# Attention products taken key tile by key tile, with the four engines' call sequences written anew, in a decoder layer on one Trainium2 core

## What is computed

```python
q, k = _l2norm(q * SCALE) * sqrt(SCALE), _l2norm(k) * sqrt(SCALE)
sim  = jnp.einsum('bhid,bjd->bhij', q, k)
attn = jax.nn.softmax(sim, axis=-1)
out  = jnp.einsum('bhij,bjd->bhid', attn, v)       # 16 heads, one k and one v
out  = out.transpose(0, 2, 1, 3).reshape(B, N, HEADS * DIM_HEAD) @ Wout
```

## Time and profile before

| | us |
|---|---|
| median of 3 timed runs | 1501.87 |
| lowest, highest of them | 1498.53, 1508.65 |
| the profiled execution's own time | 1485.55 |
| its span, first to last instruction | 1483.7 |

### The profile page before, as it was taken

One profiled execution on the slowest core, in us unless ns is written; L12 is line 12 of the kernel. 1 busy time (PEld: TensorE's weight loads), 2 busy tenths in 40 slices (PEclk: granted clock), 3 DMA queues, 4 the chain that ended last, 5 costly groups with the idle time before them and its releaser, 6 DMA issues.

```text
span 1483.7 us, 26467 instructions
## 1 busy us (share of the span) xinstructions
PE 1326.2 (89%) x6890; PEld 1021.6 (69%) x6891; DVE 1117.6 (75%) x1545; ACT 936.8 (63%) x2450; POOL 466.5 (31%) x367
## 2 busy tenths in 40 slices
PE   4699999999999999999999899998931689999996
PEld 4378885548898554889855488985421578888885
DVE  4488599959888994988899498887775347776763
ACT  4668885368878546887853688784230347666663
POOL 0001001000044211134421103461404675666664
PEclk9889999999999999999999999999965789999998
DMA  7449988632687953268796326868721369999983
GB/s 276 194 129 276 270 207 235 159 108 65 167 239 175 241 148 108 63 167 244 169 241 155 102 60 165 254 155 204 172 93 43 82 161 229 226 236 235 223 194 53
DMA packets 137517, 256.81 MB, mean 173 GB/s; under 512 B 48718, under 2 KB 50207, under 8 KB 129105
## 3 DMA queue, kind: packets, MB, share of 16 engines
q0 software_dynamic: 36480, 122.30, 36.8%
q1 hardware_dynamic: 76704, 86.70, 20.0%
q10 hardware_dynamic: 24240, 46.68, 10.0%
HBM read 166.37 MB, written 46.21 MB: 143 GB/s over the span
## 4 chain that ended last, share of the span: by engine, by line
PE 55%; DVE 13%; issue 10%; DMA 9%; ACT 5%; POOL 4%; another core or an unknown queue 1%; SPq 0%; POOLq 0%; ACTq 0%; DVEq 0%
PE bank L665 9%; PE bank L688 7%; DMA y<-dbu 4%; POOL lists L2840 4%; PE pair L537 4%; PE bank L1156 3%; PE bank L537 3%; PE bank L1157 3%; PE bank L1158 3%; PE pair L614 3%; PE pair L616 3%; PE pair L615 3%; PE bank L650 2%; PE bank L652 2%; PE bank L651 2%
## 5 line engine op out<-in xcount | busy, mean ns | idle before, releaser
L665 PE MATMUL bank<-v_aug,probs 128*128 128x129 f32 x2048 | 247.9, 277 | 6.3 <-ACT probs L1344 6.3
L665 PEld LDWEIGHTS bank<-v_aug,probs 128*128 128x128 f32 x2048 | 241.8, 193 | 15.3 <-ACT probs L1344 10.8
L2840 POOL DMA_INDIRECT lists<-entry,slot x128 | 196.7, 1537 | 136.1 <-DVE slot L2314 98.4
L688 PE MATMUL bank<-wout,o_t 128*128 128x512 f32 x512 | 231.2, 606 | 8.8 <-DMA wout<-in_wout 4.5
L1344 ACT ACTIVATE probs<-bank 128x512 f32<-128x512 f32 x256 | 152.5, 603 | 67.1 <-PE bank L665 36.1
L688 PEld LDWEIGHTS bank<-wout,o_t 128*128 128x128 f32 x512 | 98.0, 195 | 129.5 <-issue 125.0
L1353 ACT ACTIVATE decay<-delta,neg_a 128x511 f32<-128x511 f32 x256 | 164.3, 722 | 26.1 <-DVE state L2138 18.9
L2138 DVE TENSOR_TENSOR_SCAN dbu<-decay,dbu 128x1024 f32<-128x1024 f32 x64 | 144.7, 2283 | 3.2 <-ACT decay L1353 1.3
L2138 DVE TENSOR_TENSOR_SCAN state<-decay,state 128x1024 f32<-128x1024 f32 x64 | 144.5, 2281 | 1.3
L2949 POOL DMA_INDIRECT out<-y_ring,add_ids x68 | 112.6, 1656 | 79.9 <-ACT y_ring L1912 37.0
L2855 POOL DMA_DIRECT2D y<-dbu x32 | 29.2, 913 | 297.0 <-DVE dbu L2143 240.4
(11 more groups left out here) (238 smaller groups left out, 2906.1 us busy)
## 6 DMA issues: line engine op xcount, KB each, us to landing
y<-dbu POOLq DMA_DIRECT2D x32, 1024.0 KB
w_raw<-in_w_exp ACTq DMA_DIRECT2D x64, 512.0 KB
wq<-wq_dram POOLq DMA_DIRECT2D x30, 1024.0 KB
y<-state POOLq DMA_DIRECT2D x28, 1024.0 KB
wout<-in_wout SPq DMA_DIRECT2D x64, 256.0 KB, 5.6
b_bc<-bc_dram SPq DMA_DIRECT2D x64, 256.0 KB
c_bc<-bc_dram SPq DMA_DIRECT2D x64, 256.0 KB
lists<-in_const ACTq DMA_DIRECT2D x3, 2904.0 KB, 20.7
```

The costliest lines, as they stand in the source:

```text
L665: mm = pe.matmul(bank_o[half][:, (t % 2) * (DH + 1):(t % 2 + 1) * (DH + 1)], probs[:, k, t * P:(t + 1) * P], v_aug[:, k, :], start=(k == 0 ...
L688: mm = pe.matmul((bank_o + bank_s)[t][:], o_t[:, h, t * P:(t + 1) * P], wout[:, h % 4, :], start=(h == 0), stop=(h == H - 1))
L2840: pool.indirect_dma_start(out=lists, out_offset=bass.IndirectOffsetOnAxis(ap=slot[:, t, k:k + 1].bitcast(U32), axis=0), in_=entry[:, t, :] ...
```

## The change

1. `values` is called with a key tile `k` and no longer with a half. It waits for that tile's exponential only and adds its product to all four query tiles, so four accumulators are open in two banks. The waits for the banks (`o_ok` of the head before) come before its first product into each bank. Both banks end in the last call of a head, two products apart.
2. `exps(r, h, k)` waits only for `values(r, h - 1, k)`, the one that read that tile.
3. The lists of all engines are new: the same calls otherwise, in another order.
4. In VectorE's `last_row`, `split(0, 0)` and `tokens` go behind the final norm, and `split(1, 0)` goes from before the routing to behind it.
5. ScalarE, ahead of the expert part, loads the silu table itself and then executes 20 waits on `rs_seed` that have long been satisfied.

```diff
-            def values(r, h, half):
-                pe.wait_ge(S["exp_ok"], r * H * KT + h * KT + KT)
-                if h == 0:
+            def values(r, h, k):
+                pe.wait_ge(S["exp_ok"], r * H * KT + h * KT + k + 1)
+                if k == 0 and h == 0:
                     pe.wait_ge(S["v_ok"], r * 2 + 2)
                     pe.wait_ge(S["oc_ok"], r * TT)
-                else:
-                    pe.wait_ge(S["o_ok"], r * H * TT + (h - 1) * TT + 2 * half + 2)
-                for t in (2 * half, 2 * half + 1):
-                    for k in range(KT):
-                        mm = pe.matmul(bank_o[half][:, (t % 2) * (DH + 1):(t % 2 + 1) * (DH + 1)], probs[:, k, t * P:(t + 1) * P], v_aug[:, k, :],
-                                       start=(k == 0), stop=(k == KT - 1))
-                mm.then_inc(S["pv_ps"], 1)
+                for t in range(TT):
+                    if k == 0 and h > 0 and t % 2 == 0:
+                        pe.wait_ge(S["o_ok"], r * H * TT + (h - 1) * TT + t + 2)
+                    mm = pe.matmul(bank_o[t // 2][:, (t % 2) * (DH + 1):(t % 2 + 1) * (DH + 1)], probs[:, k, t * P:(t + 1) * P], v_aug[:, k, :],
+                                   start=(k == 0 and t % 2 == 0), stop=(k == KT - 1 and t % 2 == 1))
+                    if t == TT - 1 or t == 1 and k == KT - 1:
+                        mm.then_inc(S["pv_ps"], 1)
...
             def exps(r, h, k):
-                act.wait_ge(S["pv_ps"], r * H * 2 + h * 2)
+                if r + h > 0:
+                    act.wait_ge(S["pv_ps"], (r * H + h - 1) * (KT + 1) + k + 1 + k // (KT - 1))
...
+            act.preload_act_table_set("silu_and_others")
+            for done in range(1, 21):
+                act.wait_ge(S["rs_seed"], done)
             act.wait_ge(S["tab_ok"], 1)
```

More of the change, by code:

```diff
@@ L807, in first_row @@
                 q_tr(0, 1, 2)
-                head_tr(0, 2)
                 scores(0, 4, 2)
+                values(0, 4, 0)
                 scores(0, 4, 3)
+                head_tr(0, 3)
+                scores(0, 5, 0)
                 q_tr(0, 1, 3)
-                scores(0, 5, 0)
+                values(0, 4, 1)
                 scores(0, 5, 1)
-                values(0, 4, 0)
-                head_tr(0, 3)
-                values(0, 4, 1)
+                scores(0, 5, 2)
+                values(0, 4, 2)
@@ L817, in first_row @@
+                values(0, 4, 3)
                 q_piece(0, 2, 0)
-                scores(0, 5, 2)
                 scores(0, 5, 3)
                 q_piece(0, 2, 1)
-                scores(0, 6, 0)
-                head_tr(0, 4)
-                scores(0, 6, 1)
                 values(0, 5, 0)
                 values(0, 5, 1)
+                scores(0, 6, 0)
+                values(0, 5, 2)
+                values(0, 5, 3)
+                scores(0, 6, 1)
                 q_piece(0, 2, 2)
+                head_tr(0, 4)
@@ L827, in first_row @@
+                q_piece(0, 2, 3)
                 scores(0, 6, 2)
+                values(0, 6, 0)
                 scores(0, 6, 3)
-                q_piece(0, 2, 3)
-                values(0, 6, 0)
+                scores(0, 7, 0)
+                head_tr(0, 5)
                 values(0, 6, 1)
-                scores(0, 7, 0)
+                values(0, 6, 2)
                 scores(0, 7, 1)
+                values(0, 6, 3)
                 q_tr(0, 2, 0)
-                head_tr(0, 5)
                 scores(0, 7, 2)
+                q_tr(0, 2, 1)
@@ L837, in first_row @@
+                values(0, 7, 0)
                 scores(0, 7, 3)
-                q_tr(0, 2, 1)
                 q_tr(0, 2, 2)
-                values(0, 7, 0)
+                head_tr(0, 6)
+                scores(0, 8, 0)
+                q_tr(0, 2, 3)
                 values(0, 7, 1)
-                scores(0, 8, 0)
+                values(0, 7, 2)
+                values(0, 7, 3)
                 scores(0, 8, 1)
-                head_tr(0, 6)
-                q_tr(0, 2, 3)
                 scores(0, 8, 2)
+                values(0, 8, 0)
@@ L847, in first_row @@
                 scores(0, 8, 3)
-                values(0, 8, 0)
+                values(0, 8, 1)
                 head_tr(0, 7)
-                values(0, 8, 1)
+                values(0, 8, 2)
+                values(0, 8, 3)
             def row(b, r):
@@ L1031, in row @@
                 scores(r, 8, 1)
+                values(r, 7, 2)
                 q_tr(r, 2, 2)
+                head_tr(r, 6)
                 scores(r, 8, 2)
-                head_tr(r, 6)
+                values(r, 7, 3)
                 scores(r, 8, 3)
@@ L1068, in last_row @@
                 q_tr(b, 3, 1)
+                values(b, 11, 2)
                 scores(b, 12, 0)
+                head_tr(b, 10)
                 scores(b, 12, 1)
-                head_tr(b, 10)
+                values(b, 11, 3)
                 scores(b, 12, 2)
@@ L2717, in last_row @@
                 slots(b)
+                split(1, 0)
                 split_rest(1)
```

814 lines of the change are left out of this document (432 added, 382 removed).

## The result

The change makes the kernel a little slower. The median of 20 runs is 1504.62 us (1497.09 to 1513.92) against 1500.62 us (1485.70 to 1509.02) of the kernel before on the same chip. Forecast were 1496 us and a ratio of 0.9964. The time lies in the range, but only because the range also holds the time of no change; the sign is wrong.

A forecast was written before the change was run, and what follows sets the result against it. TensorE was taken to bound the four attention stretches, with 26.6 us idle to win. The terms -10 + 7 + 2.5 - 6 + 1.2 = -5.3 us gave 1496 us (ratio 0.9964), range 1486 to 1506.

The forecast's parts named there:

- Waits on `probs`, -10: In attention, TensorE's idle time before products of probabilities nearly all goes: 10 us won, bounds 0 to 10.7.
- Release of the banks, +7: Both banks end a head together, so the next head's products may wait for their division: 7 us lost, bounds 0 to 46.
- 12 tight places: Places between heads with 1.4 to 1.8 us of TensorE work before the banks are needed; 0.46 us lost at each.
- the banks' release takes it all back: Rival: the tight places between heads lose 1.4 us each, 17 us in all, so 1507 us; chance 0.20.
- The scan holds the row: Rival: VectorE and `add_state` bind at row ends, TensorE waits before the scan's projections, time near 1501; chance 0.15.
- upper bound of 46 us: Most the banks' release could cost, with a whole 2.3 us VectorE piece ahead of reciprocals at 12 and 15 places.
- Gap to `out_proj`, +2.5: At each row's end `out_proj` needs all four tiles; the gap grows from 1.24 to 1.87 us, 2.5 us lost.
- Other calls, -6: Other reordering in attention, sends and `add_state` included: 6 us won of 15.9 us idle; bounds 6 lost, 16 won.
- `split(1, 0)`, +1.2: On VectorE, its move behind the routing delays memset and block tables: 1.2 us lost, bounds 0 and 1.2.
- Fill waits and table load, 0: On ScalarE ahead of the expert part, the earlier table load and the 20 waits change nothing: 0 us.
- the rival about the loop's entry: ScalarE's stalls in the first pass of its expert loop may vanish as its program shifts: up to 8.5 us, 1488; chance 0.25.
- The new order does more: Rival: all 15.9 us of other idle goes and not 6, 10 us more won, 1486 us; chance 0.10.

The follow-up runs named there:

- half_head: adds_early with exps 0 and 1 waiting for the second key tile of the head before, exps 2 and 3 for the whole of it; ratio to before 1.002.
- after: The changed kernel itself, as traced, against the kernel before; median 1504.62 us, ratio 1.0063.
- adds_early: The changed kernel with GpSimd's accumulations of states 6 to 9 in `row` each three sends behind the last; ratio to before 0.9927.
- pool_old: The changed kernel with GpSimd's list of `row` (sends and accumulations) as it was before; ratio to before 1.0001.
- old_pool_new: The kernel before with only GpSimd's list of `row` as the change has it; ratio to before 1.007.
- the control: The kernel before run and traced once more, unchanged; ratio 1.001.
- den_first: The changed kernel with both reciprocals of head 12 moved ahead of `state_input(b, 9)` on VectorE in `row`; ratio to before 1.0107.
- no_fill: The changed kernel without its 20 fill waits, the early table load kept; ratio to before 1.0049.
- split_back: The changed kernel with `split(1, 0)` back ahead of the routing on VectorE; ratio to before 1.0037.
- ktile_old_two: The kernel before with parts 1 and 2 alone, each half replaced by two key tiles, every list in its old order; ratio to before 1.0286.

## Why the prediction was wrong, step by step

**Waits on `probs`, -10: right.** 8.5 us became 0.8. With GpSimd in time the last `out_proj` product comes 11.9 us sooner than before. (half_head shows that what the finer wait wins isn't told by these waits alone.)

**Release of the banks, +7: right in place, wrong in mechanism.** In after it is 15.8 us in 4 waits plus the clock. The sum built it from scan pieces at 12 tight places; with those alone no such wait shows (adds_early). The rival "the banks' release takes it all back" came near the time (1507 against 1504.62), but that is luck: it has small losses at 12 places, where the trace has one cause at one place in each of two rows. "The scan holds the row" named the engines of the real chain, `add_state` and VectorE's scan, and a time near 1501; but it looked for the wait at the row's end, before the scan's projections, and the trace has it at head 13. The working took free engines and pieces of 2.28 us as the longest thing in a reciprocal's way. It never asked whether the instruction ahead of the reciprocal, `state_input(b, 9)`, could itself be waiting. So even the upper bound of 46 us rested on the wrong price. The sign that it named for being wrong, a stretch of 259 us grown, is what the trace shows.

**Gap to `out_proj`, +2.5: too high.** From the start of the last product's second record to the first of `out_proj` it is 1.37, 1.37, 1.43 and 1.80 us in the four rows where it was 1.36, 1.36, 1.36 and 1.30, so 0.6 more and not 2.5. (The second trace of before has 2.44 in its last row, so even the 0.5 of that row is not sure.)

**Other calls, -6: the step that failed.** I noted that on SP and GpSimd sends and `add_state` swap by a place or two, that an accumulation is what VectorE's next but one state waits for, and then gave all of it one number with a gain's sign. No send was counted. Six more of them at 2.2 us each were moved ahead of state 7's accumulation, 13 us of queue, which made its issue 6 us later than in adds_early, and the transfer behind it took 4 us more; GpSimd's timeline of before shows how many of them stand where. GpSimd's list alone is worth 9 us between pool_old and the change (1.0001 and 1.0063), 10 between the old kernel and old_pool_new and 20 between adds_early and the change, where my bound was 6 lost. What the other idle time gave back is about 1 us by estimate (11.9 less the 10.7 of the sum), less than two traces of one kernel differ.

**`split(1, 0)`, +1.2: right,** 1.26 measured. **Fill waits and table load, 0: right** as far as 0.3% tells, and the rival about the loop's entry falls by the control. Its "no pass later stalls" was a misreading: the trace of before has 7.93 us at 1211.29. Whether they are code, as the rival supposed, no run here shows. "The new order does more", 1486 us, came about only in adds_early, which isn't the change.

**What stays open.** In the four kernels with both the new order on VectorE and the new list on GpSimd (after, den_first, no_fill, split_back) state 7's accumulation took 11.7 to 13.6 us from issue to landing, in rows 2 and 3 of each. In these eight places SP starts a load of 1 MB, `q_s<-in_x`, 0.1 to 0.2 us behind it. In the other ten traces this load starts 2.6 us or more behind it, and the accumulation took 7.5 to 11.3 us. That the load is what delays it fits, but no run moved the load alone, and so how much of the change's loss is the queue and how much this meeting isn't separated. The expert part took 312.4 to 322.8 us in six traces with the old lists and 320.8 to 331.0 in eight with the new ones. In the traces without any of ScalarE's stalls it is 312.4, 314.2 and 316.6 against 320.8 and 322.0. If that were the same in all runs, the change would have lost some 17 us instead of 4 to 9.5; adds_early, with 329.6 there, is 0.7% faster than before all the same. The traces of before are of runs some 12 to 15 us faster than the median, so I don't take the difference as shown, nor as excluded. That the rows hold most of what these kernels differ by does fit: the last `out_proj` product comes 11.9 us sooner than in the first trace of before in adds_early (0.9927), 13.2 us later in old_pool_new (1.007) and 41.5 us later in ktile_old_two (1.0286).

## What to carry to other kernels

Before an instruction is priced by its own duration and by those ahead of it in its queue, ask of each one ahead whether it waits, and for whom; a 0.16 us reciprocal behind an input that waits for a DMA costs as much as that DMA is late. When a diff swaps calls in a queue that only issues transfers, count the issues between two that someone waits for: here three sends between accumulations were free, six took 13 us of queue and brought the next accumulation out 6 us late, and the whole change turned from -0.7% to +0.6% on that list. Changing a queue also changes which transfers meet: look at what each one takes from issue to landing, not only at when it goes out. A finer dependency pays only in a sequence laid out for it: the same key tiles gave -0.7% in the new order and +2.9% in the old.

## What the runs showed that I had not expected

An idle stretch of TensorE can cost more than itself. Behind the 7.57 us stall the granted clock was 0.50 from 478.4 to about 486.4 us, by estimate another 3 us; behind the 6.11 us stall of row 3 it was 0.50 until past 752 us. Of half_head's loss in its rows the waits show less than a third; the rest is busy time at a granted clock of 0.97 instead of 0.98 to 0.99. And stalls of 3 to 8 us on ScalarE with an unknown releaser come and go between two executions of one program, with 6.4 us between the two expert parts: a single trace of before had made them look like a property of the kernel.
